# An eight-batch transformer stack on one core: wide pivot copies on ScalarE, GpSimd held back behind the normalizations, its long subtractions in halves, and new issue orders

## The reference, cut to what matters

```python
def _layernorm(x, axis=-1, eps=1e-05):
    m = jnp.mean(x, axis=axis, keepdims=True)
    v = jnp.var(x, axis=axis, keepdims=True)
    return (x - m) / jnp.sqrt(v + eps)
...
            scores = jnp.einsum('bhqd,bhkd->bhqk', q, k) / jnp.sqrt(jnp.float32(D_K))
            attn = jax.nn.softmax(scores, axis=-1)
            out = jnp.einsum('bhqk,bhkd->bhqd', attn, v)
```

## Time and profile before

| | us |
|---|---|
| median of 3 runs | 1046.17 |
| lowest and highest of them | 1043.64, 1047.5 |
| the profiled execution's own time | 1042.16 |
| its span in the profile | 1040.3 |
| PE busy in the span | 973.8 (94%) |
| VectorE busy | 667.6 (64%) |
| ScalarE busy | 561.3 (54%) |
| GpSimd busy | 221.8 (21%) |

### The profile page before, as it was taken

One profiled execution on the slowest core, in us unless ns is written; L12 is line 12 of the kernel. 1 busy time (PEld: TensorE's weight loads), 2 busy tenths in 40 slices (PEclk: granted clock), 3 DMA queues, 4 the chain that ended last, 5 costly groups with the idle time before them and its releaser, 6 DMA issues.

```text
span 1040.3 us, 17717 instructions
## 1 busy us (share of the span) xinstructions
PE 973.8 (94%) x6194; PEld 715.1 (69%) x6194; DVE 667.6 (64%) x2250; ACT 561.3 (54%) x1231; POOL 221.8 (21%) x317
## 2 busy tenths in 40 slices
PE   7989889988999999998999999999989999999998
PEld 6765655656577766776587767776577756777777
DVE  5435673577576676777575776774776566746564
ACT  1351645585457653766358643767368543773421
POOL 3004311302240051314030242212221023002210
PEclk9899999999999999999999999999999999999999
DMA  7408525221322031411313211402222004000000
GB/s 234 48 2 237 116 93 111 57 37 32 61 56 62 11 82 32 84 35 35 66 31 68 57 36 26 102 1 55 48 47 51 12 1 101 2 12 1 1 1 21
DMA packets 39927, 56.25 MB, mean 54 GB/s; under 512 B 3968, under 2 KB 35712, under 8 KB 36224
## 3 DMA queue, kind: packets, MB, share of 16 engines
q1 hardware_dynamic: 38448, 46.50, 21.8%
q10 hardware_dynamic: 1392, 8.63, 2.3%
HBM read 39.64 MB, written 13.89 MB: 51 GB/s over the span
## 4 chain that ended last, share of the span: by engine, by line
PE 57%; DVE 16%; ACT 16%; issue 7%; DMA 2%; POOL 2%; SPq 1%; ACTq 0%; DVEq 0%; POOLq 0%
PE bank L1618 7%; PE bank L1945 4%; PE bank L1478 4%; PE bank L1469 4%; PE bank L1675 4%; PE bank L1697 4%; ACT QA L841 4%; PE bank L1956 4%; ACT PT L853 3%; PE bank L1732 3%; PE bank L1590 3%; PE bank L1726 2%; PE bank L1487 2%; ACT L853 2%; PE bank L1678 2%
## 5 line engine op out<-in xcount | busy, mean ns | idle before, releaser
L853 ACT ACTIVATE PT<-bank 128x512 f32<-128x512 f32 x256 | 153.2, 598 | 143.9 <-PE bank L1678 86.6
L1675 PE MATMUL bank<-QA,KA 98*128 98x256 bf16 x512 | 113.2, 273 | 17.2 <-ACT PT L853 15.9
L1618 PE MATMUL bank<-w,xhT 128*128 128x512 f32 x256 | 126.6, 604 | 2.1 <-DVE one L1177 2.1
L1151 DVE CUSTOM_DVE_ANT_0 bank<-bank,maskb 128x256 f32<-128x256 f32 x256 | 102.0, 451 | 26.3 <-PE bank L1590 26.0
L841 ACT COPY QA<-bank 2x256 bf16<-2x256 bf16 x256 | 92.8, 363 | 24.4 <-PE bank L1656 18.4
L1144 DVE TENSOR_REDUCE mx<-bank 128x2 f32<-128x512 f32 x128 | 83.5, 682 | 32.1 <-PE bank L1590 31.4
L1590 PE MATMUL bank<-KA,QA 96*128 96x256 bf16 x512 | 91.0, 274 | 3.2 <-DVE mx L1144 1.4
L1675 PEld LDWEIGHTS bank<-QA,KA 98*128 98x128 bf16 x512 | 46.9, 99 | 64.7 <-issue 43.7
L1945 PE MATMUL bank<-xhBT,wi 128*128 128x256 f32 x336 | 87.6, 391 | 1.4 <-DVE hT L1452 0.6
L1198 DVE SCALAR_TENSOR_TENSOR x<-bank,one,x 128x256 f32<-128x256 f32 x128 | 61.5, 481 | 27.2 <-PE bank L1618 24.7
L1945 PEld LDWEIGHTS bank<-xhBT,wi 128*128 128x128 f32 x336 | 59.6, 192 | 11.5 <-DVE hT L1452 3.2
(11 more groups left out here) (316 smaller groups left out, 2093.1 us busy)
## 6 DMA issues: line engine op xcount, KB each, us to landing
QA<-scratch SPq DMA_DIRECT2D x90, 128.0 KB, 4.4
scratch<-kparts SPq DMA_DIRECT2D x30, 192.0 KB, 2.3
KA<-scratch SPq DMA_DIRECT2D x15, 384.0 KB, 4.6
scratch<-qparts SPq DMA_DIRECT2D x30, 192.0 KB, 2.3
KA<-scratch SPq DMA_DIRECT2D x15, 256.0 KB, 5.4
w<-pack ACTq DMA_DIRECT2D x1, 2409.0 KB, 8.6
wi<-ipack ACTq DMA_DIRECT2D x1, 2304.0 KB, 8.4
xin<-x_in SPq DMA_DIRECT2D x8, 256.0 KB, 5.4
```

The costliest lines, as they stand in the source:

```text
L853: act.activation(PT[:, n % RING, :, :].rearrange("p t s -> p (t s)"), st_bank[:, :], ACT.Exp).then_inc(exp_s, 1)
L1151: last = dve.tensor_tensor_reduce(s, s, maskb[:, t, :], op0=ALU.add, op1=ALU.max, scale=1.0, scalar=-HUGE, accum_out=mx[:, i % 4, n % GH, ...
L1618: last = pe.matmul(bank[n % 2][:, :], xhT[:, kk, t * P:(t + 1) * P], W("exp0", KT)[:, kk, i * 512:(i + 1) * 512], start=(kk == 0), stop=(k ...
L1675: last = pe.matmul(st_bank[:, t * S:(t + 1) * S], KA[m][0:KM, v, t * P:(t + 1) * P], QA[m][0:KM, v, :], start=True, stop=(m == 0))
```

## The change

- **Pivots.** `mq` gets one pair of neighbouring columns for each of the four heads (columns 96 to 103), one transpose brings them to rows 96 to 103 of the bank, and ACT copies all eight rows to a head with a broadcast: one copy for the first head, one for the other three. `KA` gets eight rows as well, with ones only in the two rows of its own head; they are written by `own_rows`, a copy from a small tile `rows1`, in place of the memsets. The product runs over 104 rows, not 98.
- **GpSimd waits.** After each power GpSimd waits for the scaled rows (`xh_s` or `L.s["xh"]`) before its next step.
- **GpSimd in halves.** The subtractions of `split_k` and `split_q` and the sum `x + xh` are two instructions of 256 columns each.
- **Selection.** The picks for both tiles are one `tensor_tensor` with a broadcast operand.
- **Orders.** All five strings of `TURNS` are new. They have as many letters of each thread as before, but for the filler: `w` 108 times (103 before), `z` 58 times (59 before). In VectorE's string the two steps of `own_rows` stand after the sixth and after the tenth step of `p`; the memsets stood ahead of everything. In TensorE's string 69 filler steps stand ahead of the first scores (64 before); 12 of them directly ahead of these (27 before).

```diff
-KM = KR + 2
-MQ = 32 * (GH - 1) + 2
+MR = 2 * GH
+KM = KR + MR
+MQ = KM
...
     "vector":
-        "vvpppppppppppppssssssvssssssspsssssssvvpvpvpvspspsssssssssssppssssssssssssspsbsssssssssvsssssvsspsvs"
...
+        "ppppppvppppvppppssssssssssssssssssvssvvpvpvpvspspsssssssssssppsssssssssspsssssbssssssssvsvsssssssbpv"
...
     "tensor":
-        "pwwwppwwwpwwwppwwppwwwwwwwwwwwwwwpwwwwwpwpwwwwwwppwwwwwwwwwwwwwwwwwwwwwwwwwwwsswpsspssvpsvssvsvvswww"
...
+        "pwwwpppwwwppwwwwwwwppwwwwwwwwwwwwwwwwwwwwwwwwwwwwwwpwwwwwpwpwwwwwwwwppwwwwwwwwwwwwsswpsspssvpsvswwvs"
...
+        rows1 = sb("rows1", [KM, GH], BF16)[KR:KM, :]
...
                 pool.tensor_tensor(rstd[t][:, :], veps[t][:, :], powm[:, :], ALU.pow).then_inc(rstd_s[t], 1)
+                pool.wait_ge(xh_s[t], nth(xh_s[t], b, n))
...
-                pool.tensor_tensor(kparts[:, :, 1, :], kf[:, :, :], kparts[:, :, 0, :], ALU.subtract)
-                link("p", pool.tensor_tensor(kf[:, :, :], kf[:, :, :], kparts[:, :, 0, :], ALU.subtract))
+                for k in range(KT):
+                    pool.tensor_tensor(kparts[:, k, 1, :], kf[:, k, :], kparts[:, k, 0, :], ALU.subtract)
+                for k in range(KT):
+                    last = pool.tensor_tensor(kf[:, k, :], kf[:, k, :], kparts[:, k, 0, :], ALU.subtract)
+                link("p", last)
...
-                    pool.tensor_tensor(x[:, :, :], x[:, :, :], xh[:, :, :], ALU.add).then_inc(xe_s, 1)
+                    for i in range(T):
+                        last = pool.tensor_tensor(x[:, i, :], x[:, i, :], xh[:, i, :], ALU.add)
+                    last.then_inc(xe_s, 1)
...
                 pool.tensor_tensor(rstd[t][:, lo:hi], veps[t][:, lo:hi], powm[:, lo:hi], ALU.pow).then_inc(L.s["rstd"], 1)
+                pool.wait_ge(L.s["xh"], at(L, "xh", b, n, h))
...
-                for h in range(GH):
-                    act.copy(QA[m][KR:KM, g * GH + h, :], ot_b16[32 * h:32 * h + 2, 512:512 + S]).then_inc(negm_s, 1)
+                for lo, hi in ((0, 1), (1, GH)):
+                    act.copy(QA[m][KR:KM, g * GH + lo:g * GH + hi, :],
+                             ot_b16[KR:KM, 512:512 + S].unsqueeze(1).to_broadcast([MR, hi - lo, S])).then_inc(negm_s, 1)
...
-                        high, low = (mq[:, i % 4, :, c:MQ:32] for c in range(2))
+                        high, low = (mq[:, i % 4, :, KR + c:KM:2] for c in range(2))
...
-                for t in range(T):
-                    last = dve.tensor_scalar(one[:, t, :], c1[:, t, :], cm2[:, t:t + 1], None, ALU.is_equal)
-                last.then_inc(one_s, 1)
+                dve.tensor_tensor(one[:, :, :], c1[:, :, :], cm2[:, :].unsqueeze(2).to_broadcast([P, T, E]),
+                                  ALU.is_equal).then_inc(one_s, 1)
...
+            def own_rows(m):
+                return dve.tensor_copy(KA[m][KR:KM, :, :].rearrange("p (k h) s -> p k h s", h=GH),
+                                       rows1[:, :].unsqueeze(1).unsqueeze(3).to_broadcast([MR, H // GH, GH, S]))
...
-                dve.memset(KA[0][KR:KM, :, :], 1.0).then_inc(mask_ready, 1)
-                yield
-                dve.memset(KA[1][KR:KM, :, :], 1.0).then_inc(mask_ready, 1)
+                dve.wait_ge(w_in[0], 16)
+                link("v", dve.tensor_tensor(rows1, ident[KR:KM, KR:KM:2], ident[KR:KM, KR + 1:KM:2], ALU.add))
+                own_rows(0).then_inc(mask_ready, 1)
+                yield
+                own_rows(1).then_inc(mask_ready, 1)
```

More of the change, by code:

```diff
@@ new lines @@
+        "vvssvssvsbvvbbsvpvsvsvvbsspbssbaspsvavsabvpsbbvssvppsavsbsvpsvbpvbavsspvpbbavvvavpvsbvsvsbvvsavsbvsa"
+        "vbssvsavsbvsasvbsvvbsbvsasvbbbbbbvavsvbaavssvsabasassbssvbssvvssvbasassvavvvssvvpbvvbvsvsvsvvbvbvbvc"
+        "cvvbcbbacassbassbbavssavscbsavbvbvsasvbbvsavasbbsvavbbasvsbsabvvvvbvabvvavvabvbbabvbabazbbvvbvabvavb"
+        "avvzzzzzzzzzbzzzabaaaaazzzzzaaabaaabbaaaaaaaaabaabaabaaaaaaaaaaazzzzzzzzzzzbzzzbbaaaazzzaazzbzzzbbcc"
+        "ccbbzzzzzzbbczzzzzzbbzccbbcbbzczzzzcccbcbcccbbbcbccccccccccccccccccccccccccccccc",
@@ L608, in norm_part @@
                 pool.tensor_tensor(rstd[t][:, lo:hi], veps[t][:, lo:hi], powm[:, lo:hi], ALU.pow).then_inc(rstd_s[t], 1)
+                pool.wait_ge(xh_s[t], of(xh_s[t], b, n, h))
             def split_k(b, m):
                 pool.wait_ge(k_f[m], nth(k_f[m], b, 1))
-                pool.tensor_tensor(kparts[:, :, 1, :], kf[:, :, :], kparts[:, :, 0, :], ALU.subtract)
-                link("p", pool.tensor_tensor(kf[:, :, :], kf[:, :, :], kparts[:, :, 0, :], ALU.subtract))
+                for k in range(KT):
[3 more added lines that the diff above has]
+                link("p", last)
                 yield
-                pool.tensor_tensor(kparts[:, :, 2, :], kf[:, :, :], kparts[:, :, 1, :], ALU.subtract).then_inc(k_split[m], 1)
+                for k in range(KT):
+                    last = pool.tensor_tensor(kparts[:, k, 2, :], kf[:, k, :], kparts[:, k, 1, :], ALU.subtract)
+                last.then_inc(k_split[m], 1)
                 yield
@@ L620, in split_q @@
                 pool.wait_ge(q_f[m], nth(q_f[m], b, 1))
-                pool.tensor_tensor(parts[:, :, 1, :], f[:, :, :], parts[:, :, 0, :], ALU.subtract)
-                link(t, pool.tensor_tensor(f[:, :, :], f[:, :, :], parts[:, :, 0, :], ALU.subtract))
+                for k in range(KT):
+                    pool.tensor_tensor(parts[:, k, 1, :], f[:, k, :], parts[:, k, 0, :], ALU.subtract)
+                for k in range(KT):
+                    last = pool.tensor_tensor(f[:, k, :], f[:, k, :], parts[:, k, 0, :], ALU.subtract)
+                link(t, last)
                 yield
-                pool.tensor_tensor(parts[:, :, 2, :], f[:, :, :], parts[:, :, 1, :], ALU.subtract).then_inc(q_split[m], 1)
+                for k in range(KT):
+                    last = pool.tensor_tensor(parts[:, k, 2, :], f[:, k, :], parts[:, k, 1, :], ALU.subtract)
+                last.then_inc(q_split[m], 1)
                 yield
@@ L1356, in top2 @@
                     link(L.t, dve.tensor_reduce(L.m2[:, lo:hi], L.r2[:, lo:hi, :], AX.X, ALU.max))
-                    for t in range(lo, hi):
-                        last = dve.tensor_scalar(L.pick2[:, t, :], L.r2[:, t, :], L.m2[:, t:t + 1], None, ALU.is_equal)
-                    link(L.t, last)
+                    link(L.t, dve.tensor_tensor(L.pick2[:, lo:hi, :], L.r2[:, lo:hi, :],
+                                                L.m2[:, lo:hi].unsqueeze(2).to_broadcast([P, hi - lo, E]), ALU.is_equal))
                     link(L.t, dve.scalar_tensor_tensor(L.r3[:, lo:hi, :], L.pick2[:, lo:hi, :], -4.0, L.r3[:, lo:hi, :],
@@ L1364, in top2 @@
                                                    ALU.is_lt, ALU.mult))
-                for t in range(lo, hi):
-                    last = dve.tensor_scalar(L.r2[:, t, :], L.r2[:, t, :], L.m1[:, t:t + 1], None, ALU.mult)
-                link(L.t, last)
+                link(L.t, dve.tensor_tensor(L.r2[:, lo:hi, :], L.r2[:, lo:hi, :],
+                                            L.m1[:, lo:hi].unsqueeze(2).to_broadcast([P, hi - lo, E]), ALU.mult))
                 dve.tensor_tensor(L.tw[:, lo:hi, 0:E * R].rearrange("p t (e r) -> p t e r", r=R),
@@ L1649, in tops @@
                 if i:
-                    pe.wait_ge(negm_s, i * GH)
+                    pe.wait_ge(negm_s, 2 * i)
                 if g == 0 and q:
@@ L1670, in value @@
                             i = n // GH
[L1671 removed]
+                            pe.wait_ge(negm_s, 2 * (n // GH) + (1 if n % GH == 0 else 2))
                             if n:
```

70 lines of the change are left out of this document (32 added, 38 removed).

## The result

| | before | after |
|---|---|---|
| median of the runs, us | 1045.64 (4 runs) | 996.62 (4 runs) |
| lowest and highest | 1043.64, 1047.5 | 995.81, 998.81 |
| profiled execution, own time and span | 1042.16, 1040.3 | 996.77, 995.0 |
| granted TensorE clock | 0.987 | 0.997 |

The ratio is 0.9535, with a 95% interval of 0.951 to 0.956: 49 us less, 4.7%. The forecast was 1033 us, 1.3% less. The direction was right. The size was not: the time lies 17 us under the low end of the range.

What follows compares the result with a forecast made beforehand. TensorE (PE), 94% busy, was taken as the bound, its waits as the gain. Terms summed to -20.0 us, two thirds kept (-13.3): 1028.8 profiled, 1033 us as median; own range 1022 to 1040, whole range 1014 to 1049.

Steps and rivals of the forecast that it cites:

- The waits: GpSimd held behind VectorE's scalings: collisions go, 11.7 us of PE's 15.6 us of waits won, before the discount.
- The cost in the last batch: Second half's GpSimd power comes behind the first half's scaling, 5 pairs by about 0.4 us: counted +1.0 us.
- The halves: GpSimd instructions of 256 columns: shorter collisions for pivots and pick, -2.0 us; longer splits for the first batches, +0.8.
- The pivots: ACT's pivot copies: 0.280 us less per group, 17.9 us of ACT, 45% on the chain, so 8.0 us.
- The picks: Fused picks on VectorE: 29 fewer instructions, 5.5 us of VectorE, only the choice ahead of PE, so -1.0 us.
- The start: Memsets moved behind the first statistics: first scores at 39.5 to 40.4, counted nothing (-1.5 if copy cheap, +3 if 7 us).
- The orders: New order strings of all engines: counted 0, with 8 us to each side.
- The discount of a third: On the whole sum: an earlier PE meets its next wait, so two thirds of -20.0 us survive, -13.3.
- The gaps only move: Rival: PE's other waits, exponential or score rows, take up the gain; 1041 to 1051 us, chance 0.14.
- GpSimd becomes late: Rival: held GpSimd delays the read-back of query and key rows, scores start late; slower, 1055 us, chance 0.08.
- the order alone costs: Rival: new order makes PE wait once more per batch for maxima or exponentials; 1051 to 1060 us, chance 0.08.
- More than forecast: Rival: the order closes gaps too and the sum of 20 us holds whole; 1014 to 1022 us, chance 0.12.

Runs made afterwards that it cites:

- e7: The kernel before with only the three GpSimd waits added, instructions of 512 columns and old order kept: 1033.79 us, ratio 0.992.
- e3: The kernel after without the three GpSimd waits behind the scalings: 1002.11 us, ratio 0.961.
- e11: The kernel after with the old pivots (columns 32 apart, 98 rows, four copies) and the old order: 1023.14 us, ratio 0.982.
- e2: The kernel after with all five old order strings, all code edits kept: 1007.61 us, ratio 0.967.
- e1: The kernel before with only the five new order strings: 1035.15 us, ratio 0.990.
- e4: The kernel after with GpSimd's halves joined again into instructions of 512 columns, waits kept: 997.53 us, ratio 0.956.
- e12: The kernel after without the GpSimd waits and with whole instructions of 512 columns: 1008.23 us, ratio 0.969.
- e8: The kernel after with the picks of choose and top2 separate for each tile again: 999.31 us, ratio 0.958.
- e10: The kernel after with the old pivots (columns 32 apart, 98 rows, four copies, memsets at the places of own_rows), new order: 1021.32 us, ratio 0.980.
- e13: As e10, but all four pivot copies of a group read rows 0 and 1, the first head's pivot: 1002.12 us, ratio 0.961.
- e5: The kernel after with four pivot copies of 8x256 for each group, new layout kept: 1000.28 us, ratio 0.960.
- e17: The kernel before, old order, with only the new pivots and their own_rows: 1025.35 us, ratio 0.985.
- e16: The kernel after with one more 8x256 copy in each group, to a tile nothing reads: 1009.13 us, ratio 0.969.
- e9: The kernel after without GpSimd waits or halves, with four pivot copies and separate picks (new order and layout stay): 1019.30 us, ratio 0.979.
- e14: As e10, but all four pivot copies read rows 96 and 97, where they also write: 1004.33 us, ratio 0.963.

## Why the prediction was right in direction and too small

**The waits: right.** I had 15.6 us of PE's waits and 11.7 of it, after the discount 7.8. The waits gave 6.5 to 8.5 alone (e7) and 5.5 as the last edit (e3). The row that I had named, scalings at 0.40 to 0.42 without exception, is there but for some at 0.38. The cost in the last batch (+1.0) can't be told apart.

**The halves: right in what they cost, wrong in what they bring.** GpSimd's busy time rose by 13.4 us, to 235.2 (13 forecast); a half takes 0.67 (0.65 forecast). The halves of `kparts` in the kernel after, by shape:

```profile
L617 POOL TENSOR_TENSOR kparts<-kf,kparts 128x256 bf16<-128x256 f32 x32 | 20.9, 674 | 90.1 <-ACT kf L756 72.1 <-DVE xh L1065 17.9
```

Their worth is 0.9 us beside the waits and 6.1 without them. I had counted 2.0 us for them, by PE's waits for the pivots and the pick. Those waits are gone, but the halves did not do it. PE waits for `mq` 2.0 us in the kernel before, 2.4 and 2.1 with halves in the old order (e11, e2), and 0.3 at most in every kernel with the new order, also with whole instructions (e1, e4, e12): it was the order. The wait for `one` is 2.1 before, 0.7 with halves and separate picks (e8), and none with whole instructions and fused picks (e4, e12): it was mostly the fused pick. What the halves do is to cover for the waits, which I had not counted.

**The pivots: this is the step that failed.** The mechanism was right, that shorter pivot copies on ACT let the exponentials come earlier, and the sum "0.280 less, in 64 groups 17.9 us of ACT" by "45%" was mis-sized in both factors.
- The first factor: a group of the kernel before holds ACT for 1.523 us and not 1.452, and one of the kernel after for 1.061 and not 1.172. That is 0.462 less, 29.6 us in 64 groups. Shown by e10, e13 and e5: 22.5 of the 29.6 come with the layout, by the place that is read, and 7.1 from the joined copy.
- The second factor: the share of the copies on the chain, 41.6 of 92.8, was taken as the price of a microsecond, and then cut to two thirds, together 0.3. Measured it is 0.5 in the old order (e17, and e11 to e2) and 0.7 to 0.8 in the new one (e16, e10 to e13, and e10 to after; up to 0.9 by the ratios). A likely reason, argued and not shown: the chain names one line for each moment, and holds only what ended last in this one schedule, while shorter copies also bring forward the exponentials that come close behind it.

Together 16 to 25 us for the pivots where 5.3 stood in the forecast (8.0 by two thirds).

**The picks:** 2.7 us by the medians, 5 by the ratios, against 1.0, not resolved; PE's waits for them are 0.7 us for `one` and 1.5 for `tw` in e8, and none in the kernel after. The fused pick in the kernel after, ns min/median/max:

```profile
L1194 DVE TENSOR_TENSOR one<-c,cm x8: 174/176/683, 78.8 to 791.2; 128x16 f32<-128x16 f32 x8
```

Two of the eight are longer, 0.68 and 0.60 us, both beside a GpSimd instruction in flight. The Trainium skill ("SBUF — State Buffer", Who interferes with whom) says that a VectorE instruction with two inputs in SBUF contends with a GpSimd instruction that reads SBUF. The trace agrees for these two; four others of the eight start with a GpSimd instruction in flight and take 0.17 to 0.18. The separate picks of e8 are hit more often: eight of their sixteen take 0.60 to 0.80. So the fused form, which I had held to be still exposed, is the less exposed one here, and not every VectorE instruction that meets a GpSimd instruction stands still, as I had read from the earlier trace rows.

**The start:** the copy is 2.29 us where 3.5 was taken, and with the first scores 3.1 us earlier the cheap case of my bound (-1.5) is the nearest, though this start moves by more than that between like kernels.

**The orders: a bound too narrow.** They are worth 10 to 11 us, where I had 0 with 8 to each side. Of the 22 us of gap in the middle stretch the kernel with the new order alone closes little by itself (PE 399.0 of 420, e1), but in it PE also works through more of the program in the same time:

```profile
200.00:620.00 420.00, 399.04 (x2592) 293.73 (x2591) 296.64 (x1021) 256.38 (x547) 97.33 (x133) 0.99 0.25 49
```

2592 matmuls against 2568. In e1 PE waits 8.1 us for scaled rows in place of 15.6, and 19.2 for the exponential in place of 15.9. Where GpSimd's waits already take care of the scalings and the copies are the old ones, the order is worth only 1.8 us (e11 to e10), less than is told apart (e10 also has its memsets at the late places); with the new copies it is worth 11 (e2 to after). So the order and the shorter copies belong together. Which of its moves does it was not tried.

**The discount of a third.** I argued that a PE that comes earlier meets its next wait. For the waits it was about right: 7.8 against 5.5 to 8.5. For the pivots it was wrong: they are worth as much beside the other code edits (15.5, e11 to e2) as alone (16, e17), and 9 us more in the new order (24.7, e10 to after). There the discount had the wrong sign, since the next wait was the exponential and the pivot copies stand in front of it. That is not so between all edits. Taken out one at a time (e3, e4, e5, e8) four of them cost 5.5 + 0.9 + 3.7 + 2.7 = 12.8 us, and all four together (e9) 22.7: singly they cost little, since the rest covers for the one that is missing. For the waits and the halves e3, e4 and e12 show that pair by pair; for the copies and the picks only this sum speaks.

**The rivals.** "The gaps only move" failed: the wait that should have taken the gain fell too. "GpSimd becomes late" and "the order alone costs" failed: e7 and e1 are faster than before. "More than forecast" came nearest, with the first of its two reasons (the order closes gaps) right, and its 1014 to 1022 still 17 us short, since it too had the copies at 17.9 us of ACT.

**The clock.** The granted clock by slice, in the kernel before and then in the kernel after:

```profile
PEclk9899999999999999999999999999999999999999
```

```profile
PEclk9999989999999999999999999999999999999999
```

The mean rose from 0.987 of 1040.3 us to 0.997 of 995.0, which is 13.5 us of full speed missing before and 3.0 now. In the kernel after one stretch is left at 0.50, the lower of the two levels (1.2 in place of 2.4 GHz), behind a stretch in which PE stood still:

```profile
124.00:126.00 2.00, 0.00 (x0) 0.00 (x0) 0.00 (x0) 1.47 (x3) 0.00 (x0) 0.84 0.87 166
...
125.40:132.20 6.80, 5.89 (x24) 4.18 (x25) 3.78 (x19) 1.59 (x4) 0.00 (x0) 0.50 0.14 39
```

The kernels with fewer PE waits show the higher clock (e10 0.988, e13 0.995), so a part of the gain is paid through the clock. How large it is can be read from the executions of the kernel before alone. In the 53 of them that ran beside the experiments the time falls from 1051.5 us at a clock of 0.977 to 1036.81 and 1037.0 at 0.997, about 0.7 us for each 0.001. The kernel after took 995.81 to 996.77 at 0.997. At the same clock 40 of the 49 us are left, so about 9 came with the clock. The same comparison leaves about 5 us of the 10 for the order alone (e1 took 1032.35 to 1034.85 at 0.992, the kernel before 1038.32 to 1040.56), 14 to 15 of the 16 for the pivots alone (e17 took 1024.19 and 1024.64 at 0.992), and 5.5 for the waits alone (e7 took 1032.67 to 1033.95 at 0.990, the kernel before 1039.11 and 1039.23). Within one program it is not shown whether the lower clock makes the time or a longer pause makes both. My sum had no term for the clock.

## What to carry to other kernels

Cost a run of small instructions by the distance from start to start in the timeline, never by the sum of their durations: here copies of nearly the same length (0.363 and 0.361 us) stood 0.386 apart in one layout and 0.27 in the other, and that was the largest single part of the gain. On a kernel whose bound engine waits for one other engine, its share of the chain that ended last can be a poor price for a saving: here it gave 0.45 and the runs 0.5 to 0.8, as the exponentials stood behind the copies. Before discounting a sum, ask for each pair of edits whether one shortens the wait that the other runs into (here the order and the shorter copies: more together) or whether both remove the same wait (here GpSimd's waits and halves: less together). When two kernels differ in granted clock, compare executions at the same clock as well.

## What the runs showed of the hardware that I had not expected

- **ACT's overlap depends on the rows that are read.** Two-row copies out of the bank that read one place take 0.355 to 0.360 us each and start 0.27 apart; the same copies, each from a place 32 rows further on, start 0.386 apart (e10 against e13 and e14, nothing else changed). Between copies that write to the same rows it is the place read that decides, and not the number of rows (8 in e5, 0.27 too) or whether the copy reads the rows that it writes to (e14, 0.27 too). Where an instruction of 128 rows written from row 0 on follows a pivot copy in e13, the 24 ns stand between them although both read from row 0 on.
- **A wider copy of ones is the faster one.** On VectorE a broadcast copy of 8x4096 bf16 takes 2.29 us, the memset of 2x4096 took 3.47.
- **The collision with GpSimd grows with the length of its instruction.** The maximum of the scalings of thread `s` is 1.24 with instructions of 512 columns (e12), 0.81 with 256 (e3), and 0.415 if GpSimd is held back (after). The Trainium skill ("SBUF — State Buffer", Who interferes with whom) says that the engine that starts first holds the shared ports for its whole instruction; the trace agrees, with 1.24, 0.81 and 0.415 us.
